# A two-layer graph attention kernel: the loop's order of steps on four engines laid out anew

## Chip, cores and metric

The kernel runs on one NeuronCore of a Trainium2 chip. The metric is the device time of one launch in microseconds (us). Before the change it is 1103.05 us, the median of 3 runs (1102.35 to 1104.42).

## What is computed

Two attention layers over 64 graphs of 128 nodes with 384 features, each followed by a residual sum and a layer norm. The first has 6 heads of 64 and a dot-product softmax; the second has 12 heads of 32 with additive attention, an ELU and a gate.

```python
def _L0_gnn_ref(seq_inputs, Wq, bq, Wk, bk, Wv, bv, Wf, bf, graph_mask):   # 6 heads of 64
    q = _heads(seq_inputs @ Wq + bq)
    k = _heads(seq_inputs @ Wk + bk)
    v = _heads(seq_inputs @ Wv + bv)
    scores = jnp.einsum('bhqd,bhkd->bhqk', q, k) / np.sqrt(HEAD_SIZE)
    bias = jnp.where(graph_mask, 0.0, NEG)[:, None]
    probs = jax.nn.softmax(scores + bias, axis=-1)
    ctx = jnp.einsum('bhqk,bhkd->bhqd', probs, v)
    ...
    return ctx @ Wf + bf

def _L1_gnn_ref(feat_in, adj, W, b, w_src, w_dst, H_w, H_b):               # 12 heads of 32
    h = jnp.einsum('bnd,ade->bane', feat_in, W)
    th = jnp.tanh(h)
    attn_src = jnp.einsum('bane,aeo->bano', th, w_src)
    attn_dst = jnp.einsum('bane,aeo->bano', th, w_dst)
    attn = attn_src + jnp.swapaxes(attn_dst, 2, 3)
    attn = jnp.where(attn >= 0, attn, LEAKY_ALPHA * attn)
    attn = jnp.where(mask, jnp.float32(-999.0), attn)
    attn = jax.nn.softmax(attn, axis=-1)
    feat_out = jnp.einsum('banm,bame->bane', attn, h) + b
    ...
    feat_out = jax.nn.elu(feat_out)
    gate = jax.nn.sigmoid(feat_in @ H_w.T + H_b)
    return gate * feat_out + (1.0 - gate) * feat_in

x = _layernorm(x + _L0_gnn_ref(x, ..., adj), axis=-1)      # x: 64 x 128 x 384, adj: 64 x 128 x 128
x = _layernorm(x + _L1_gnn_ref(x, adj, ...), axis=-1)
```

## The kernel before

The 64 graphs go through in 16 groups of 4. Weights and inputs are split into a high and a low part (the `hi` and `lo` steps), and each projection is 9 matmuls: 3 slices of the features by 3 products of parts (`project`, L577). The work of a group is cut into some 70 named steps on each engine, and every step carries the number of a graph in the group or of a part of one: `("qk", 3)` is the fourth of the six query and key projections, `("wb", 7)` the eighth of twelve blocks of second-layer logits.

The program has three phases: a beginning, a loop of 13 turns (`Fori(1, NG - 2)` with `NG` = 16) and an end. The order in which an engine does its steps is written out by hand in tables: `PE_LOOP`, `ACT_LOOP`, `DVE_LOOP` and `POOL_LOOP` for a turn of the loop, and others for the beginning and the end. In one turn the second layer works on group u, the first layer on group u + 1, and the transposes of the inputs (`xT`, `xhi`, `xlo`) on group u + 2. No engine reorders anything: a step that waits holds up all that stands behind it in its table.

Steps wait for each other by semaphores, one to a kind of step. Besides the data, TensorE (PE) waits for banks. All transposes and the `wb` blocks go to two PSUM banks in turn (`t_bank`, the kinds in `T_STAGES`), all projections to two others (`p_bank`, the kinds in `P_STAGES`). A step takes the bank of the step two places ahead of it among its kinds, so it waits until that one's result was read (`bank`, and the tables `t_freed` and `p_freed`). A change of the order thus also changes who waits for whom.

Steps that the prediction speaks of, with their lines:

- PE: `v`, `qk`, `h`, `gate`, `f` (L577), `xT` (L609), `s` (L639), `pT` (L648), `pv0` (L660), `maskT` (L678), `x1T` (L686), `qwT` (L707), `wb` (L716), `pv1` (L730 and L736), `sumsT` (L750).
- ScalarE (ACT): `qkout` (L801, reads `qk`), `pTo` (L827), `chi` (L833), `hout` (L846, L848), `sumsTo` (L853), `gatet` (L858), `pqw` (L864 to L867), `qwhi` (L876), `qwTo` (L883), `elu` (L890, L894), `exp` (L818), `xhi` (L787).
- VectorE (DVE): `sda` (L1018), `wlog` (L1022), `mixa`, `mixb`, `sum1` (L1064, L1069, L1075), `e` (L1042), `f_raw` (L1057, frees the bank of `sumsT`), and `xlo`, `x1lo`, `clo`, `qwlo`, all by the helper `low` (L920).
- GpSimd (POOL): `prod` (L1142), `rows` (L1149, makes `w_rows` for three `wb`), `norm` (L1130), `fb` (L1154), `ex` (L1160), `rstd` (L1111, L1113).

The second layer's chain for a graph: `h`, `hout`, `prod`, `sd`, `sda`, `wlog`, `pqw`, `qwhi`, `qwlo`, `qwT`, `qwTo`, `rows`, `wb`, `e`, `pv1`, `sumsTo`, `sumsT`, `f_raw`, `fb`, `elu`, `ex`, `mixa`, `mixb`, `sum1`.

Of the kernel before, what the change touches and what calls it, by code (L numbers as in the profile page):

```python
# [25 lines left out]

PE_LOOP = [
# [8 lines left out]
]  # L36

PE_BEGIN = [
# [37 lines left out]
]  # L76

ACT_LOOP = [
    ("vout", 0), ("masks", 0), ("x1hi", 0), ("qkout", 0), ("qkout", 1), ("qkout", 2), ("hout", 0), ("x1hi", 1),
    ("pqw", 0), ("qwhi", 0), ("qkout", 3), ("hout", 1), ("qwTo", 0), ("qkout", 4), ("gatet", 0), ("qkout", 5),  # L80
    ("pqw", 1), ("qwhi", 1), ("x1hi", 2), ("qwTo", 1), ("gatet", 1), ("exp", 0), ("vout", 1), ("hout", 2),
    ("sumsTo", 0), ("x1hi", 3), ("exp", 1), ("elu", 0), ("hout", 3), ("pTo", 0), ("pTo", 1), ("pqw", 2), ("pTo", 2),
    ("qwhi", 2), ("sumsTo", 1), ("pTo", 3), ("pqw", 3), ("chi", 0), ("qwhi", 3), ("qwTo", 2), ("exp", 2), ("vout", 2),
    ("qwTo", 3), ("exp", 3), ("chi", 1), ("pTo", 4), ("pTo", 5), ("vout", 3), ("elu", 1), ("sumsTo", 2), ("gatet", 2),
    ("chi", 2), ("pTo", 6), ("elu", 2), ("sumsTo", 3), ("pTo", 7), ("chi", 3), ("xhi", 0), ("xhi", 1), ("elu", 3),
    ("xhi", 2), ("xhi", 3), ("gatet", 3),
]

# [33 lines left out]
]  # L122

DVE_LOOP = [
    ("x1lo", 0), ("gsum", 0), ("x1lo", 1), ("sd", 0), ("sda", 0), ("wlog", 0), ("qwlo", 0), ("sd", 1), ("sda", 1),
    ("wlog", 1), ("qwlo", 1), ("gsum", 1), ("x1lo", 2), ("mask", 0), ("e", 0), ("max", 0), ("e", 1), ("e", 2),
    ("mask", 1), ("e", 3), ("e", 4), ("e", 5), ("rden0", 0), ("max", 1), ("rden1", 0), ("x1lo", 3), ("f_raw", 0),
    ("sd", 2), ("sda", 2), ("rden0", 1), ("wlog", 2), ("gsum", 2), ("mask", 2), ("max", 2), ("sd", 3), ("sda", 3),
    ("qwlo", 2), ("wlog", 3), ("mixa", 0), ("mixb", 0), ("qwlo", 3), ("sum1", 0), ("rden1", 1), ("clo", 0),
    ("stats1", 0), ("mask", 3), ("mv1", 0), ("rden0", 2), ("f_raw", 1), ("max", 3), ("e", 6), ("e", 7), ("e", 8),  # L130
    ("sum0", 0), ("stats0", 0), ("clo", 1), ("rden0", 3), ("mv0", 0), ("e", 9), ("e", 10), ("e", 11), ("mixa", 1),
    ("rden1", 2), ("f_raw", 2), ("mixb", 1), ("sum0", 1), ("clip", 0), ("clo", 2), ("stats0", 1), ("out", 0),
    ("x1", 0), ("sum1", 1), ("clip", 1), ("mv0", 1), ("stats1", 1), ("sum0", 2), ("mixa", 2), ("rden1", 3),
    ("mv1", 1), ("f_raw", 3), ("mixb", 2), ("clo", 3), ("stats0", 2), ("xlo", 0), ("sum1", 2), ("mv0", 2),
    ("gsum", 3), ("xlo", 1), ("x1", 1), ("stats1", 2), ("sum0", 3), ("xlo", 2), ("mv1", 2), ("xlo", 3), ("mixa", 3),
    ("stats0", 3), ("mixb", 3), ("out", 1), ("mv0", 3), ("sum1", 3), ("stats1", 3), ("mv1", 3), ("out", 2), ("x1", 2),
    ("x1", 3), ("out", 3),
]

# [55 lines left out]
POOL_LOOP = [  # L195
    ("prod", 0), ("prod", 1), ("rows", 0), ("rows", 1), ("x_res", 0), ("prod", 2), ("norm", 0), ("fb", 0),
    ("norm", 1), ("prod", 3), ("ex", 0), ("rows", 2), ("norm", 2), ("rows", 3), ("fb", 1), ("norm", 3), ("ex", 1),
    ("rstd1", 0), ("rstd0", 0), ("fb", 2), ("ex", 2), ("rstd0", 1), ("fb", 3), ("rstd1", 1), ("rstd0", 2), ("ex", 3),
    ("rstd1", 2), ("rstd0", 3), ("rstd1", 3),
]  # L200

# [1009 lines left out]
```

## Time and profile before

| what | us |
|---|---|
| median of 3 runs | 1103.05 |
| the profiled execution, whole | 1102.98 |
| its span, first to last instruction | 1101.1 |
| PE busy | 1057.9 (96%) |
| VectorE busy | 872.4 (79%) |
| GpSimd busy | 704.2 (64%) |
| ScalarE busy | 651.4 (59%) |
| chain that ended last | PE 79%, VectorE 12%, issue 6% |

The span is time from the first to the last instruction; what lies around it is 1.9 us. Busy time of PE is modelled: the records of neighbouring matmuls overlap, and a short wait for a bank does not show as idle time. The distance from the start of one step to the start of the next does show it. The granted clock of TensorE is 1.00 in every turn of the loop. DMA moves 28 GB/s over the span.

### The profile page before, as it was taken

The numbers are of one execution on the slowest core, as the hardware profiler recorded it, in microseconds if no ns is written. First come the engines' busy times: TensorE is split into PE (matmuls) and PEld (weight loads), VectorE is DVE, ScalarE is ACT, GpSimd is POOL, SyncE is SP. The second block draws the span as 40 slices with busy tenths as digits, with TensorE's granted clock in tenths as the row PEclk, the third lists the DMA queues.
The fourth block names the chain that finished last, engine by engine and source line by source line (L and its number), as shares of the span: only waits on it lengthen the run. The fifth ranks groups of instructions, "written<-read, shape, count | busy, mean of one in ns | idle before, by whom it ended". The sixth has DMA issues, their size and how long they took to land.

```text
span 1101.1 us, 28478 instructions
## 1 busy us (share of the span) xinstructions
PE 1057.9 (96%) x9226; PEld 894.6 (81%) x9226; DVE 872.4 (79%) x2289; ACT 651.4 (59%) x2060; POOL 704.2 (64%) x605
## 2 busy tenths in 40 slices
PE   6999999999999999999999999999999999999974
PEld 4888888888888888888888888888888888888853
DVE  3659779696887969789696987969789696977977
ACT  4747466474755647566475755647565575746532
POOL 0347577575766758477575757758577574866765
PEclk9999999999999999999999999999999999999988
DMA  6101010000101001010000101001010100100000
GB/s 189 32 1 33 30 33 9 22 30 29 31 29 31 7 21 31 29 31 14 22 30 21 31 29 31 7 21 31 29 31 19 38 9 21 31 29 2 9 16 37
DMA packets 34722, 31.00 MB, mean 28 GB/s; under 512 B 15872, under 2 KB 34688, under 8 KB 34688
## 3 DMA queue, kind: packets, MB, share of 16 engines
q1 hardware_dynamic: 34688, 30.57, 9.0%
q8 instruction: 19, 0.31, 0.1%
q14 instruction: 15, 0.12, 0.0%
HBM read 17.98 MB, written 12.58 MB: 28 GB/s over the span
## 4 chain that ended last, share of the span: by engine, by line
PE 79%; DVE 12%; issue 6%; ACT 1%; POOL 1%; DMA 0%; DVEq 0%; POOLq 0%; ACTq 0%
PE p_bank L577 50%; PE t_bank L716 4%; PE context L730 4%; DVE weights L1042 4%; PE scores L639 4%; PE context L736 4%; PE t_bank L648 3%; PE context L660 3%; PE t_bank L609 2%; PE t_bank L750 2%; PE t_bank L686 2%; DVE sd L1011 1%; DVE masked L950 1%; DVE neg_max L958 1%; PE t_bank L707 1%
## 5 line engine op out<-in xcount | busy, mean ns | idle before, releaser
L1149 POOL TENSOR_TENSOR w_rows<-qwT,own_head 96x1536 fp32r<-96x1536 f32 x64 | 179.8, 2809 | 87.8 <-ACT qwT L883 87.8
L1042 DVE SCALAR_TENSOR_TENSOR weights<-t_bank,pqw,clip 128x128 f32<-128x128 f32 x768 | 206.5, 343 | 7.4 <-PE t_bank L716 6.7
L1142 POOL TENSOR_TENSOR prod<-th,w_sd 128x768 f32<-128x768 f32 x64 | 118.3, 1848 | 124.9 <-ACT th L846 124.8
L818 ACT ACTIVATE probs<-masked,neg_max 128x128 f32<-128x128 f32 x384 | 148.8, 391 | 46.4 <-DVE neg_max L958 46.4
L577 PE MATMUL p_bank<-xT,w_q 128*128 128x512 f32 x432 | 113.7, 408 | 4.3 <-DVE w_k L927 4.3
L577 PE MATMUL p_bank<-w_v,xT 128*128 128x384 f32 x576 | 115.1, 344 | 1.2 <-DVE clip L995 1.2
L577 PE MATMUL p_bank<-w_f,cT 128*128 128x384 f32 x576 | 115.4, 344 | 0.4 <-DVE cT L920 0.4
L577 PE MATMUL p_bank<-w_h,x1T 128*128 128x384 f32 x576 | 113.8, 342 | 0.2 <-DVE x1T L920 0.2
L577 PE MATMUL p_bank<-w_g,x1T 128*128 128x384 f32 x576 | 113.1, 340 | 0.0
L577 PE MATMUL p_bank<-xT,w_k 128*128 128x512 f32 x432 | 111.4, 402 | 0.0
L1130 POOL TENSOR_TENSOR probs<-probs,rden 128x768 f32<-128x768 f32 x64 | 94.4, 1475 | 25.0 <-DVE rden L963 25.0
L577 PEld LDWEIGHTS p_bank<-w_h,x1T 128*128 128x128 f32 x576 | 101.2, 189 | 6.2 <-issue 2.6
L577 PEld LDWEIGHTS p_bank<-w_v,xT 128*128 128x128 f32 x576 | 99.7, 188 | 5.3 <-issue 3.4
L577 PEld LDWEIGHTS p_bank<-w_g,x1T 128*128 128x128 f32 x576 | 100.9, 188 | 2.0
L577 PEld LDWEIGHTS p_bank<-w_f,cT 128*128 128x128 f32 x576 | 99.0, 188 | 1.7 <-DVE cT L920 1.0
L577 PEld LDWEIGHTS p_bank<-xT,w_q 128*128 128x128 f32 x432 | 80.2, 191 | 24.4 <-DVE w_k L927 4.7
L1154 POOL TENSOR_TENSOR f_b<-f_raw,bias 128x384 f32<-128x384 f32 x64 | 71.3, 1114 | 40.2 <-DVE f_raw L1057 40.1
L1160 POOL TENSOR_TENSOR elu_steps<-elu_steps,x 128x384 f32<-128x384 f32 x64 | 74.9, 1170 | 30.0 <-ACT elu_steps L894 27.2
L1011 DVE TENSOR_REDUCE sd<-prod 128x24 f32<-128x768 f32 x64 | 60.4, 944 | 41.7 <-POOL prod L1142 41.7
L577 PEld LDWEIGHTS p_bank<-xT,w_k 128*128 128x128 f32 x432 | 79.5, 189 | 16.2
L716 PE MATMUL t_bank<-w_rows,qwT 96*128 96x512 f32 x192 | 84.6, 468 | 5.8 <-ACT probs0T L827 2.1
L1113 POOL TENSOR_TENSOR rstd<-ve,minus_half 128x1 f32<-128x1 f32 x128 | 79.1, 618 | 10.0
(109 smaller groups left out, 2279.9 us busy)
## 6 DMA issues: line engine op xcount, KB each, us to landing
x_in<-in_x_dram SPq DMA_DIRECT2D x16, 768.0 KB, 4.7
out_dram<-y_out SPq DMA_DIRECT2D x64, 192.0 KB, 1.9
adj_in<-in_adj_dram SPq DMA_DIRECT2D x16, 64.0 KB, 4.3
probs0T<-in_L_gnn_Wq_dram SPq DMA_DIRECT2D x1, 576.0 KB, 6.2
weights<-in_L_gnn_Wk_dram SPq DMA_DIRECT2D x1, 576.0 KB, 7.3
x_res<-in_L_gnn_Wv_dram SPq DMA_DIRECT2D x1, 576.0 KB, 7.4
probs<-in_L_gnn_Wf_dram SPq DMA_DIRECT2D x1, 576.0 KB, 7.4
x<-in_L_gnn_W_dram SPq DMA_DIRECT2D x3, 192.0 KB, 6.1
```

The source lines that it names most:

```text
L577: last = te.matmul(dst, left(a, kt), right(b, kt), start=(n == 0), stop=(n == 3 * KT - 1))
L639: last = te.matmul(scores[:, b, j * P:(j + 1) * P], head(qT, j, b, k), head(kT, j, b, k), start=True, stop=True)
L716: te.matmul(dst[:, :], qwT[:, g % 2, 0, :], w_rows[0:QW_ROWS, g % 2, heads, :].rearrange("p h i -> p (h i)"), start=True, stop=True).then_ ...
L818: last = act.activation(probs0[:, k % 2, b, j * P:(j + 1) * P], masked[:, k % 2, b * PAIRS + j, :], ACT.Exp, bias=neg_max[:, b * PAIRS + j ...
L1011: dve.tensor_reduce(sd[:].rearrange("p a h -> p (a h)"), prod[:].rearrange("p a (h e) -> p (a h) e", h=H1), AX_X, ALU.add).then_inc(s_sd, 1)
L1042: last = dve.scalar_tensor_tensor(out=weights[:, g % 2, n, :], in0=src[:, i * P:(i + 1) * P], scalar=pqw[:, g % 2, 0, n:n + 1], in1=clip[: ...
L1113: pool.tensor_tensor(rstd, ve, minus_half[:], ALU.pow).then_inc(made_rstd, 1)
L1130: pool.tensor_tensor(probs, probs, per_head(rden0[:], P), ALU.mult).then_inc(s_norm, 1)
L1142: pool.tensor_tensor(prod[:], over_heads(th[:], 2), w_sd[:], ALU.mult).then_inc(s_prod, 1)
L1149: pool.tensor_tensor(w_rows[0:QW_ROWS, k % 2], over_heads(qwT[:, k % 2, 1, :].bitcast(F32), H1), per_head(own_head[:], P), ALU.mult).then_ ...
L1154: pool.tensor_tensor(f_b[:, k % 2, :].rearrange("p (h e) -> p h e", h=H1), f_raw[:].rearrange("p (h e) -> p h e", h=H1), over_heads(bias_1 ...
L1160: pool.tensor_tensor(exp_less_x, f_exp, x1[:, k, :], ALU.subtract).then_inc(s_ex, 1)
```

## The change

No instruction is added, removed or altered. The four loop tables are permuted; those of the beginning and the end stay. The new order was laid out for the mean over four randomly shifted sets of durations. In ACT's table, besides what stands below, `gatet` 1 goes behind `sumsTo` 0, `gatet` 2 ahead of `exp` 3, `pTo` 6 ahead of `chi` 2, and `elu` 3 ahead of `xhi` 1. At PE's end `xT` 2 goes ahead of `f` 3, and in DVE's table `stats1` 2 ahead of `xlo` 1. Some lines of the difference:

```diff
 PE_LOOP = [
...
-    ("qwT", 0), ("qk", 4), ("x1T", 2), ("qk", 5), ("gate", 1), ("s", 0), ("qwT", 1), ("wb", 0), ("v", 1), ("wb", 1),
+    ("qk", 4), ("qwT", 0), ("qk", 5), ("x1T", 2), ("gate", 1), ("s", 0), ("wb", 0), ("qwT", 1), ("v", 1), ("wb", 1),
...
-    ("pv1", 1), ("h", 3), ("pT", 0), ("s", 2), ("pT", 1), ("pT", 2), ("pT", 3), ("pv0", 0), ("s", 3), ("qwT", 2),
-    ("sumsT", 1), ("v", 2), ("qwT", 3), ("f", 0), ("wb", 6), ("wb", 7), ("v", 3), ("wb", 8), ("pv0", 1), ("pT", 4),
+    ("pv1", 1), ("pT", 0), ("h", 3), ("s", 2), ("pT", 1), ("pT", 2), ("pT", 3), ("pv0", 0), ("s", 3), ("sumsT", 1),
+    ("qwT", 2), ("v", 2), ("qwT", 3), ("f", 0), ("wb", 6), ("wb", 7), ("v", 3), ("wb", 8), ("pv0", 1), ("pT", 4),
...
 ACT_LOOP = [
...
-    ("pqw", 0), ("qwhi", 0), ("qkout", 3), ("hout", 1), ("qwTo", 0), ("qkout", 4), ("gatet", 0), ("qkout", 5),
+    ("qkout", 3), ("pqw", 0), ("qwhi", 0), ("hout", 1), ("qwTo", 0), ("qkout", 4), ("qkout", 5), ("gatet", 0),
...
 DVE_LOOP = [
...
-    ("rden1", 2), ("f_raw", 2), ("mixb", 1), ("sum0", 1), ("clip", 0), ("clo", 2), ("stats0", 1), ("out", 0),
+    ("sum0", 1), ("clip", 0), ("rden1", 2), ("mixb", 1), ("f_raw", 2), ("stats0", 1), ("mv0", 1), ("clo", 2),
...
 POOL_LOOP = [
...
-    ("rstd1", 0), ("rstd0", 0), ("fb", 2), ("ex", 2), ("rstd0", 1), ("fb", 3), ("rstd1", 1), ("rstd0", 2), ("ex", 3),
+    ("rstd1", 0), ("rstd0", 0), ("fb", 2), ("ex", 2), ("rstd1", 1), ("fb", 3), ("rstd0", 1), ("ex", 3), ("rstd0", 2),
```

PE, the first quarter of a turn, from `("h", 1)` to the step behind `("s", 0)`. Before:

```order
L577 MATMUL p_bank1<-w_h,x1T 128x384 x9
L707 MATMUL t_bank0<-ident,qw_parts 96x128 x2
L467 REGISTER_ALU
L577 MATMUL p_bank0<-xT,w_q 128x512 x9
L683 REGISTER_ALU
L686 MATMUL t_bank1<-ident,x1 128x128 x3
L577 MATMUL p_bank1<-xT,w_k 128x512 x9
L467 REGISTER_ALU
L577 MATMUL p_bank0<-w_g,x1T 128x384 x9
L634 REGISTER_ALU
L639 MATMUL scores<-kT,qT 128x128 x6
L707 MATMUL t_bank0<-ident,qw_parts 96x128 x2
L716 MATMUL t_bank1<-w_rows,qwT 128x512
```

Now:

```order
L577 MATMUL p_bank1<-w_h,x1T 128x384 x9
L467 REGISTER_ALU
L577 MATMUL p_bank0<-xT,w_q 128x512 x9
L707 MATMUL t_bank0<-ident,qw_parts 96x128 x2
L577 MATMUL p_bank1<-xT,w_k 128x512 x9
L683 REGISTER_ALU
L686 MATMUL t_bank1<-ident,x1 128x128 x3
L467 REGISTER_ALU
L577 MATMUL p_bank0<-w_g,x1T 128x384 x9
L634 REGISTER_ALU
L639 MATMUL scores<-kT,qT 128x128 x6
L716 MATMUL t_bank0<-w_rows,qwT 128x512
```

The transposes of `qw_parts` (`qwT` 0 and 1) each go one matmul step later: the first behind a `qk` projection, the second behind the first block of `w_rows` logits (`wb` 0). With it the banks of these two swap.

VectorE, the middle of a turn: `qw_parts` is `qwlo` (2, then 3), `mix` is `mixa` and `mixb`, `sum1` and `stats1` belong to the first graph's second layer norm. Before (`f_raw` 1 stands three rows behind the last):

```order
L920 TENSOR_TENSOR qw_parts<-pqw,qw_parts 128x2x12
L1022 TENSOR_SCALAR wlog<-sda 128x12
L1064 SCALAR_TENSOR_TENSOR mix<-f_b,elu_steps 128x384
L1069 SCALAR_TENSOR_TENSOR mix<-gate_t,mix 128x384
L1024 REGISTER_ALU
L920 TENSOR_TENSOR qw_parts<-pqw,qw_parts 128x2x12
L1075 SCALAR_TENSOR_TENSOR sum1<-mix,x1 128x384
L1050 RECIPROCAL rden1<-t_bank0 128x4x3
L920 TENSOR_TENSOR cT<-context0,cT 128x384
L1079 BN_STATS stats1<-sum1 128x6
L945 REGISTER_ALU
L950 TENSOR_TENSOR masked<-scores,neg 128x768
```

Now:

```order
L1064 SCALAR_TENSOR_TENSOR mix<-f_b,elu_steps 128x384
L1024 REGISTER_ALU
L920 TENSOR_TENSOR qw_parts<-pqw,qw_parts 128x2x12
L1022 TENSOR_SCALAR wlog<-sda 128x12
L1069 SCALAR_TENSOR_TENSOR mix<-gate_t,mix 128x384
L1050 RECIPROCAL rden1<-t_bank1 128x4x3
L1075 SCALAR_TENSOR_TENSOR sum1<-mix,x1 128x384
L1024 REGISTER_ALU
L920 TENSOR_TENSOR qw_parts<-pqw,qw_parts 128x2x12
L920 TENSOR_TENSOR cT<-context0,cT 128x384
L1057 TENSOR_TENSOR f_raw<-t_bank1,rden1 128x384
```

`mixa` goes ahead of `qwlo` 2, `sum1` ahead of `qwlo` 3, and `f_raw` 1 comes ahead of `stats1`.

PE, the last fifth of a turn, from behind `("pv1", 3)` to `("pv0", 3)`. Before:

```order
L678 MATMUL t_bank1<-ident_b,adj_b 128x128 x2
L467 ISA
L648 MATMUL t_bank0<-ident,probs0 128x128 x3
L577 MATMUL p_bank1<-w_f,cT 128x384 x9
L467 REGISTER_ALU
L750 MATMUL t_bank1<-ident,sumsT 128x128 x4
L652 REGISTER_ALU
L660 MATMUL context0<-probs0T,v 64x128 x6
```

Now:

```order
L648 MATMUL t_bank1<-ident,probs0 128x128 x3
L467 REGISTER_ALU
L678 MATMUL t_bank0<-ident_b,adj_b 128x128 x2
L577 MATMUL p_bank1<-w_f,cT 128x384 x9
L467 REGISTER_ALU
L750 MATMUL t_bank1<-ident,sumsT 128x128 x4
L660 MATMUL context0<-probs0T,v 64x128 x6
```

`pT` 7 and `maskT` 1 swap, so `sumsT` 3 now takes the bank of `pT` 7 and no longer that of `maskT` 1.

## Rows read from the trace of the kernel before

**Rows 1.** The page: span, then busy us (share of the span) xinstructions.
```profile
span 1101.1 us, 28478 instructions
...
PE 1057.9 (96%) x9226; PEld 894.6 (81%) x9226; DVE 872.4 (79%) x2289; ACT 651.4 (59%) x2060; POOL 704.2 (64%) x605
```
**Rows 2.** Stretches: us, PE, PEld, DVE, ACT, POOL busy, clock, DMA share, GB/s.
```profile
451.80:517.60 65.80, 65.13 (x576) 55.35 (x575) 53.67 (x143) 40.20 (x129) 44.04 (x38) 1.00 0.08 25
...
978.00:1101.10 123.10, 101.71 (x904) 82.01 (x901) 97.91 (x259) 57.29 (x179) 77.62 (x68) 0.93 0.05 19
```
**Rows 3.** Timeline, PE, first third: start us, us, instruction, count, [idle <-releaser].
```profile
465.66 1.73 PE L577 MATMUL p_bank<-w_h,x1T 128*128 128x384 f32 x9
467.29 0.42 PE L707 MATMUL t_bank<-ident,qw_parts 128*96 128x128 f32 x2
467.64 2.38 PE L577 MATMUL p_bank<-xT,w_q 128*128 128x512 f32 x9
...
474.82 0.42 PE L707 MATMUL t_bank<-ident,qw_parts 128*96 128x128 f32 x2
475.34 0.47 PE L716 MATMUL t_bank<-w_rows,qwT 96*128 96x512 f32 x1
```
**Rows 4.** Timeline, ACT, the same place.
```profile
466.92 0.67 ACT L801 ACTIVATE kT<-p_bank,bias_q 128x512 f32<-128x512 f32 x1
```
**Rows 5.** Timeline, DVE: the second `sda` of the turn.
```profile
471.02 1.64 DVE L1018 TENSOR_TENSOR sda<-sd,sd_shift 128x24 f32<-128x24 f32 x1
```
**Rows 6.** Timeline, POOL: `rows` 0, 2 and 3, `fb` 1 and 2.
```profile
469.86 2.76 POOL L1149 TENSOR_TENSOR w_rows<-qwT,own_head 96x1536 fp32r<-96x1536 f32 x1
...
494.27 3.00 POOL L1149 TENSOR_TENSOR w_rows<-qwT,own_head 96x1536 fp32r<-96x1536 f32 x1 [2.14 <-ACT qwT L883]
...
498.66 2.75 POOL L1149 TENSOR_TENSOR w_rows<-qwT,own_head 96x1536 fp32r<-96x1536 f32 x1
501.38 1.00 POOL L1154 TENSOR_TENSOR f_b<-f_raw,bias 128x384 f32<-128x384 f32 x1
...
507.73 1.25 POOL L1154 TENSOR_TENSOR f_b<-f_raw,bias 128x384 f32<-128x384 f32 x1 [0.60 <-DVE f_raw L1057]
```
**Rows 7.** Timeline, PE, middle of the turn.
```profile
493.03 0.42 PE L707 MATMUL t_bank<-ident,qw_parts 128*96 128x128 f32 x2
493.29 0.60 PE L750 MATMUL t_bank<-ident,sumsT 128*128 128x128 f32 x4
```
**Rows 8.** Timeline, DVE, the same place.
```profile
492.72 0.18 DVE L920 TENSOR_TENSOR qw_parts<-pqw,qw_parts 128x24 fp32r<-128x24 f32 x1
...
492.91 0.56 DVE L1064 SCALAR_TENSOR_TENSOR mix<-f_b,elu_steps 128x384 f32<-128x384 f32 x1
...
493.98 0.18 DVE L920 TENSOR_TENSOR qw_parts<-pqw,qw_parts 128x24 fp32r<-128x24 f32 x1
494.10 0.56 DVE L1075 SCALAR_TENSOR_TENSOR sum<-mix,x 128x384 f32<-128x384 f32 x1
...
496.61 0.52 DVE L1057 TENSOR_TENSOR f_raw<-t_bank,rden 128x384 f32<-128x384 f32 x1
```
**Rows 9.** Timeline, PE, `qwT` 3, `f` 0 and the two `wb` behind it.
```profile
495.31 0.38 PE L707 MATMUL t_bank<-ident,qw_parts 128*96 128x128 f32 x2
495.45 1.83 PE L577 MATMUL p_bank<-w_f,cT 128*128 128x384 f32 x9
497.32 0.74 PE L716 MATMUL t_bank<-w_rows,qwT 96*128 96x512 f32 x2
```
**Rows 10.** Timeline, ACT, last `probs0T` copy of the turn.
```profile
510.63 0.48 ACT L827 ACTIVATE probs0T<-t_bank 128x384 f32<-128x384 f32 x1
```
**Rows 11.** Timeline, PE, end of the turn: `sumsT` 3, then `xT` 2 and 3.
```profile
511.60 0.60 PE L750 MATMUL t_bank<-ident,sumsT 128*128 128x128 f32 x4
...
516.82 0.82 PE L609 MATMUL t_bank<-ident,x_in 128*128 128x128 f32 x6
```
**Rows 12.** Timeline, DVE, `xlo` 1.
```profile
516.38 0.55 DVE L920 TENSOR_TENSOR xT<-t_bank,xT 128x384 fp32r<-128x384 f32 x1
```

More of the change, by code:

```diff
@@ L78 @@
 ACT_LOOP = [
-    ("vout", 0), ("masks", 0), ("x1hi", 0), ("qkout", 0), ("qkout", 1), ("qkout", 2), ("hout", 0), ("x1hi", 1),
-    ("pqw", 0), ("qwhi", 0), ("qkout", 3), ("hout", 1), ("qwTo", 0), ("qkout", 4), ("gatet", 0), ("qkout", 5),
[L81 to L85, printed above, removed]
+    ("x1hi", 0), ("vout", 0), ("qkout", 0), ("masks", 0), ("qkout", 1), ("qkout", 2), ("hout", 0), ("x1hi", 1),
+    ("qkout", 3), ("pqw", 0), ("qwhi", 0), ("hout", 1), ("qwTo", 0), ("qkout", 4), ("qkout", 5), ("gatet", 0),
+    ("pqw", 1), ("x1hi", 2), ("qwhi", 1), ("qwTo", 1), ("exp", 0), ("vout", 1), ("hout", 2), ("sumsTo", 0),
+    ("gatet", 1), ("x1hi", 3), ("exp", 1), ("elu", 0), ("hout", 3), ("pTo", 0), ("pTo", 1), ("sumsTo", 1), ("pqw", 2),
+    ("pTo", 2), ("pTo", 3), ("qwhi", 2), ("chi", 0), ("pqw", 3), ("qwhi", 3), ("qwTo", 2), ("exp", 2), ("qwTo", 3),
+    ("vout", 2), ("gatet", 2), ("exp", 3), ("chi", 1), ("pTo", 4), ("pTo", 5), ("vout", 3), ("elu", 1), ("sumsTo", 2),
+    ("pTo", 6), ("chi", 2), ("elu", 2), ("sumsTo", 3), ("pTo", 7), ("chi", 3), ("xhi", 0), ("elu", 3), ("xhi", 1),
     ("xhi", 2), ("xhi", 3), ("gatet", 3),
@@ L124 @@
 DVE_LOOP = [
-    ("x1lo", 0), ("gsum", 0), ("x1lo", 1), ("sd", 0), ("sda", 0), ("wlog", 0), ("qwlo", 0), ("sd", 1), ("sda", 1),
-    ("wlog", 1), ("qwlo", 1), ("gsum", 1), ("x1lo", 2), ("mask", 0), ("e", 0), ("max", 0), ("e", 1), ("e", 2),
-    ("mask", 1), ("e", 3), ("e", 4), ("e", 5), ("rden0", 0), ("max", 1), ("rden1", 0), ("x1lo", 3), ("f_raw", 0),
+    ("x1lo", 0), ("x1lo", 1), ("gsum", 0), ("sd", 0), ("sda", 0), ("wlog", 0), ("qwlo", 0), ("sd", 1), ("sda", 1),
+    ("wlog", 1), ("gsum", 1), ("x1lo", 2), ("qwlo", 1), ("mask", 0), ("e", 0), ("max", 0), ("e", 1), ("e", 2),
+    ("mask", 1), ("e", 3), ("rden0", 0), ("e", 4), ("e", 5), ("max", 1), ("rden1", 0), ("x1lo", 3), ("f_raw", 0),
     ("sd", 2), ("sda", 2), ("rden0", 1), ("wlog", 2), ("gsum", 2), ("mask", 2), ("max", 2), ("sd", 3), ("sda", 3),
-    ("qwlo", 2), ("wlog", 3), ("mixa", 0), ("mixb", 0), ("qwlo", 3), ("sum1", 0), ("rden1", 1), ("clo", 0),
-    ("stats1", 0), ("mask", 3), ("mv1", 0), ("rden0", 2), ("f_raw", 1), ("max", 3), ("e", 6), ("e", 7), ("e", 8),
-    ("sum0", 0), ("stats0", 0), ("clo", 1), ("rden0", 3), ("mv0", 0), ("e", 9), ("e", 10), ("e", 11), ("mixa", 1),
-    ("rden1", 2), ("f_raw", 2), ("mixb", 1), ("sum0", 1), ("clip", 0), ("clo", 2), ("stats0", 1), ("out", 0),
[L133 to L136, printed above, removed]
+    ("mixa", 0), ("qwlo", 2), ("wlog", 3), ("mixb", 0), ("rden1", 1), ("sum1", 0), ("qwlo", 3), ("clo", 0),
[4 rows of a table added]
+    ("rden1", 3), ("f_raw", 3), ("mixb", 2), ("clo", 3), ("xlo", 0), ("stats0", 2), ("sum1", 2), ("gsum", 3),
+    ("stats1", 2), ("xlo", 1), ("mv0", 2), ("xlo", 2), ("x1", 1), ("mv1", 2), ("sum0", 3), ("xlo", 3), ("mixa", 3),
+    ("stats0", 3), ("mixb", 3), ("out", 1), ("x1", 2), ("sum1", 3), ("mv0", 3), ("out", 2), ("stats1", 3), ("mv1", 3),
     ("x1", 3), ("out", 3),
```

11 rows, old and new, of tables (DVE_LOOP, PE_LOOP) are left out of this document.

## The prediction

> **What bounds it.** I read the page first: the span is 1101.1 us and TensorE (PE) is busy for 1057.9 of it, 96% [rows 1]. Nothing else is near that, and PE does not get less work, so the change can give back only what PE waits. The table of stretches comes next: a turn of the loop takes 65.80 us at a granted clock of 1.00, and the 13 turns are 855 us of the span; the rest, like the 123.1 us behind the loop, keeps its order [rows 2]. Busy time cannot show the short waits, so I went through one turn in the timeline and took the distance from each step's start to the next one's. Where two steps of one kind differ there, the longer one holds a wait. For example `qwT` 3 (at 495.31) lets `f` 0 start 0.14 us later, while `qwT` 0 (467.29) holds the next step back for 0.35 and `qwT` 1 (474.82) for 0.52 [rows 3, 9]. I found about 2.7 us of such waits in a turn. All of them gone would be 13 x 2.7 = 35 us, the ceiling. The question is how many go and how many come back elsewhere.
>
> **The change, place by place.** Each term is us per turn.
>
> First third, `qk` 4. It starts at 467.64, 0.05 behind the end of the `kT` copy that frees its bank (466.92 + 0.67 = 467.59) [rows 3, 4]. ScalarE makes that copy behind `pqw` 0 and `qwhi` 0, though its input was there at about the start of `h` 1, 465.66. Now `qkout` 3 goes ahead of these two, and `qk` 4 goes straight behind `h` 1. `qwT` 0 sits between two projections and should cost 0.14 instead of 0.35, and `h` 1 no longer ends in a wait for `qwlo` 0 (under 0.1). Bounds: -0.21 (the transpose alone) and -0.4 (with the refill behind a wait at `qk` 4). I take -0.3. `qwlo` 0 and `qwTo` 0 come later, and `rows` 0 with them by about 0.4, but `wb` 0 starts at 475.34 and `rows` 0 ended at 472.62 [rows 3, 6], so 2.7 us cover it.
>
> `wb` 0 and `qwT` 1. The 0.38 that `qwT` 1 holds too long is a wait for `x1lo` 2, which frees the bank of `wb` 0. In the new order `wb` 0 fills most of that time, but `qwlo` 1 now comes behind `x1lo` 2 on VectorE, so `qwT` 1 waits for it instead, and `wb` 1 takes the bank of `wb` 0 and so waits for `e` 0. One wait becomes two shorter ones. Between -0.3 (all hidden) and +0.3 (both last as long as the old one); I take 0.
>
> Middle, `qwT` 2 to `wb` 6. `mixa` 0 goes ahead of `qwlo` 2, which moves that 0.5 us back (a `mix` is 0.56 long, with 0.1 overlapped) [rows 8]. Before, `qwT` 2 started at 493.03, 0.13 behind the end of `qwlo` 2 (492.90), and `sumsT` 1 followed at 493.29 [rows 7, 8]; now `sumsT` 1 goes first and fills the time, so `qwT` 2 comes about where it was. Then `qwT` 3 takes the bank of `sumsT` 1, which `f_raw` 1 frees. Before, `f_raw` 1 ended at 497.13, 1.8 behind the start of `qwT` 3 [rows 8, 9]. It is moved ahead of `stats1`, `mask` 3, `mv1` and `rden0`, 1.5 us of work, so it ends at about 495.2 to 495.6, while PE would be ready for `qwT` 3 at 494.9 to 495.0. That is a new wait of 0.2 to 0.6. It costs less than that, because `f` 0 to `wb` 6 is 1.87 where a 384-wide projection needs 1.6 to 1.7: there PE waited for `rows` 2, which ended at 497.27, 0.05 ahead of `wb` 6 at 497.32 [rows 6, 9]. The two waits share one slack. `rows` 2 itself took 3.00 against 2.75 for `rows` 3 [rows 6]; it ran beside `sum1` 0 (494.10 to 494.66) [rows 8], which reads two tiles of SBUF, and now `sum1` 0 starts about 0.5 ahead of it. So `wb` 6 can come 0.3 earlier, or 0.2 later if `f_raw` 1 comes at the late end. I take -0.15.
>
> From `wb` 6 to `f` 1 PE's order is the same. VectorE gets to `max` 3 some 0.1 to 0.2 sooner, as `mv1` 0 goes behind `e` 8, and the `wb` and `pT` blocks here wait for `e` and for `pTo`: 0 to -0.25, I take -0.1.
>
> End, `sumsT` 3. It takes the bank of `pT` 7, so it now waits for the last `probs0T` copy. That ended at 511.11, and `sumsT` 3 started at 511.60 [rows 10, 11]: 0.49 of slack. Two things move it. `f_raw` 2 goes behind `sum0` 1, `clip` 0 and `mixb` 1, about 1.3 us of steps, of which VectorE's idle time ahead of the old place and its head start cover 0.8 to 1.0; and the chain `fb` 2, `elu` 2, `sumsTo` 3, `pTo` 7 hangs on it. Against it, `fb` 2 took 1.25 beside `mixb` 1 where `fb` 1 took 1.00 [rows 6], and it no longer runs beside `mixb`. The copy then ends at 511.1 to 511.6 on the old clock, while PE with its gains would be there at 511.1. Cost 0 to +0.5; I take +0.2.
>
> Seam, `xT` 3. It waits for `xlo` 1, which ended at 516.93, while `xT` 2 and 3 started at 516.82 and some 0.33 later [rows 11, 12]. VectorE now does `stats1` 2 ahead of `xlo` 1, and ScalarE does `elu` 3 ahead of `xhi` 1. Slack of 0.2 against a delay of 0 to 0.5: 0 to +0.3, I take +0.05.
>
> **Sum.** -0.3 + 0 - 0.15 - 0.1 + 0.2 + 0.05 = -0.3 us a turn, times 13 is -3.9. The profiled execution is 1102.98 us, its span and 1.9 around it, and 0.07 under the median of 1103.05. So 1102.98 - 3.9 = 1099.1 us. This forecast holds for -0.1 to -0.45 a turn, 1097.1 to 1101.7. All terms at their best ends are -1.25 (1086.7) and all at their worst +1.1 (1117.3), but a PE that comes late at one place waits less at the next, so neither sum is likely.
>
> **A collision that could turn it.** VectorE's second `sda` of a turn has 24 elements a row and took 1.64 us [rows 5], where a `qw_parts` of the same size takes 0.18 [rows 8]. It ended at 472.66, 0.04 behind the end of `rows` 0 at 472.62 [rows 5, 6]. So a VectorE instruction with two operands in SBUF that comes while a large GpSimd one runs is held until that one's end. `qwlo` reads two tiles in SBUF too. In the new order `qwlo` 3 stands behind `sum1` 0 and comes at almost the same moment as `rows` 2 starts: before, `qwlo` 3 began at 493.98 and `rows` 2 at 494.27, 0.29 later [rows 6, 8]; `sum1` 0 in front moves it back by 0.46, so now they are within 0.1 of each other. If `rows` 2 is first, `qwlo` 3 waits for up to 2.75 us, and `qwT` 3, `f` 0 and all behind it with it.
> The Trainium skill (SBUF — State Buffer, section "SBUF: two separate sides") calls the pair of ports that the two engines share an exclusive lock: whichever starts first has it for its whole instruction and the other fully blocks. The trace agrees for `sda`, 1.64 against 0.18. By that rule a start of `rows` 2 ahead of `qwlo` 3 makes the slow case below, 1132 us.
> What speaks against it: `sum1` 0 starts well before `rows` 2 and the next VectorE instruction follows it with no gap, so VectorE may keep the port through both.
>
> **Rivals.**
> 1. The end gives it back. `sumsT` 3 waits for `pTo` 7 and `xT` 3 for `xlo` 1, both in full: +0.5 and +0.3 in place of +0.2 and +0.05 makes -0.3 + 0.55 = +0.25; with the shared slack between the two taken off, about +0.1 a turn, 1104.3, and 1101.7 to 1106 as its range. For it: ScalarE's order at that place is `elu`, `sumsTo`, `pTo` with nothing to overtake. Against: the shorter `fb` 2.
> 2. The waits in the middle go further than I take: `wb` 1, `qwT` 3 and `wb` 6 all at their better ends, -0.6 a turn, 1095.2. For it: the ceiling is 2.7. Against: each has a new releaser only a little ahead.
> 3. The collision at `qwlo` 3, the slower side. `rows` 2 ends 2.75 after its start, `qwT` 3 comes at about 497.1 instead of 495.3, and `clo` 0, `f_raw` 1 and the whole of VectorE's work behind it are late by 2.5. PE loses 2.0 to 2.6 a turn: 13 x 2.3 = 30, less the 1 us or so of gain ahead of it, 1132. It decides on whether `rows` 2 starts before `qwlo` 3.
>
> That the tables would not do what they say is excluded: each engine's order is the table's.
>
> **Chances.** Forecast 0.40, rival 1 0.33, rival 2 0.17, rival 3 0.10. About 0.2%, 2.2 us, is what a measurement of this kernel can tell from no change, so faster means below 1100.8 and slower above 1105.3. Faster: 0.34 of the forecast's 0.40 and all of rival 2, 0.51. Same: 0.06 and 0.20 of rival 1, 0.26. Slower: 0.13 of rival 1 and rival 3, 0.23. The range 1094.5 to 1108 takes in the forecast, rival 1 and the nearer part of rival 2; it leaves out rival 3.
>
> **What would show it.** The stretch of one turn should be 65.5 instead of 65.80, with a clock of 1.00 as before. `h` 1 to `qk` 4 should be 1.6 with no wait, and `qwT` 0 0.14 long. `qwT` 3 should start within 0.1 of the end of `f_raw` 1, and `rows` 2 take 2.75 to 2.85. `sumsT` 3 should start either right behind the last `probs0T` copy (rival 1) or clear of it. A `qwlo` of over 1 us anywhere is rival 3. I am wrong if the turn is above 65.7 with `sumsT` 3 clear of its copy, or if the difference lies outside the 13 turns.

## The result, and the profile after

The changed kernel takes 1106.43 us (median of 20 runs, 1105.07 to 1108.19), the kernel before 1102.94 on the same chip (20 runs). The ratio is 1.0031 with a 95% interval of 1.0024 to 1.0038: slower by 0.31%, where 0.35% faster was forecast (1102.98 to 1099.1). The profiled execution has a span of 1104.5 us.

The page after, span and busy times, against [rows 1]:
```profile
span 1104.5 us, 28473 instructions
...
PE 1061.7 (96%) x9221; PEld 890.1 (81%) x9226; DVE 875.1 (79%) x2289; ACT 656.7 (59%) x2060; POOL 682.5 (62%) x605
```
The table of stretches after (columns as in [rows 2]), the same turn and the part behind the loop:
```profile
452.90:518.96 66.06, 65.45 (x574) 54.99 (x574) 53.85 (x143) 40.56 (x128) 42.32 (x38) 1.00 0.08 25
981.30:1104.50 123.20, 101.11 (x898) 81.94 (x901) 97.51 (x259) 57.01 (x178) 76.59 (x68) 0.94 0.05 19
```
A turn is 66.06 us instead of 65.80, and the part behind the loop 123.2 instead of 123.1. The loss is in the 13 turns: 13 x 0.28 = 3.6 us. Below, "turn" is the mean of the last ten: 65.78 before, 66.06 after. The last of them leads into the end phase and is some 0.2 shorter (65.61 and 65.84), so the turns in the middle of the loop are 65.80 and 66.08. POOL is busy for 22 us less and the time is not shorter for it.

To see where in the turn, I took the start of each TensorE step behind the start of its turn's `v` 0 (median over the last ten turns) and cut the turn at steps that stand in the same place in both orders:

| stretch | predicted | before | after | difference |
|---|---|---|---|---|
| turn start to `h` 1 | 0 | 13.90 | 13.90 | 0.00 |
| `h` 1 to `s` 0 | -0.3 | 8.29 | 8.01 | -0.28 |
| `s` 0 to `wb` 3 | 0 | 6.38 | 6.51 | +0.13 |
| `wb` 3 to `s` 3 | 0 | 11.63 | 11.55 | -0.08 |
| `s` 3 to `wb` 6 | -0.15 | 5.35 | 5.51 | +0.16 |
| `wb` 6 to `f` 1 | -0.1 | 7.30 | 7.20 | -0.10 |
| `f` 1 to `sumsT` 3 | +0.2 | 6.98 | 7.09 | +0.11 |
| `sumsT` 3 to the next turn | +0.05 | 5.95 | 6.29 | +0.34 |

The eight differences sum to +0.28, where -0.3 was forecast.

The first third did what was forecast. The timeline of TensorE after, against [rows 3]: `qk` 4 straight behind `h` 1, `qwT` 0 only 0.13 ahead of `qk` 5; then `wb` 0 and `qwT` 1.
```profile
468.36 2.26 PE L577 MATMUL p_bank<-xT,w_q 128*128 128x512 f32 x9
470.46 0.38 PE L707 MATMUL t_bank<-ident,qw_parts 128*96 128x128 f32 x2
470.59 2.35 PE L577 MATMUL p_bank<-xT,w_k 128*128 128x512 f32 x9
...
475.65 0.50 PE L716 MATMUL t_bank<-w_rows,qwT 96*128 96x512 f32 x1
476.18 0.42 PE L707 MATMUL t_bank<-ident,qw_parts 128*96 128x128 f32 x2
```
`qwT` 1 starts at 476.18, 0.06 behind the end of `qwlo` 1 in VectorE's timeline after (475.95 + 0.17 = 476.12), and `sda` 1, held by `rows` 0 before for 1.64 [rows 5], is now held for 2.13, again until the end of `rows` 0 (471.42 + 2.75 = 474.17):
```profile
472.09 2.13 DVE L1018 TENSOR_TENSOR sda<-sd,sd_shift 128x24 f32<-128x24 f32 x1
...
475.95 0.17 DVE L920 TENSOR_TENSOR qw_parts<-pqw,qw_parts 128x24 fp32r<-128x24 f32 x1
```
Middle of the turn after, against [rows 7 to 9]. TensorE (`v` 2, `qwT` 3, `f` 0):
```profile
494.56 1.83 PE L577 MATMUL p_bank<-w_v,xT 128*128 128x384 f32 x9
496.57 0.39 PE L707 MATMUL t_bank<-ident,qw_parts 128*96 128x128 f32 x2 [0.17 <-DVE f_raw L1057]
496.72 1.81 PE L577 MATMUL p_bank<-w_f,cT 128*128 128x384 f32 x9
```
VectorE, the same place (`sum1` 0, `qwlo` 3, and behind `clo` 0 `f_raw` 1), and POOL's `rows` 2:
```profile
494.86 0.53 DVE L1075 SCALAR_TENSOR_TENSOR sum<-mix,x 128x384 f32<-128x384 f32 x1
495.31 0.18 DVE L920 TENSOR_TENSOR qw_parts<-pqw,qw_parts 128x24 fp32r<-128x24 f32 x1
...
495.87 0.55 DVE L1057 TENSOR_TENSOR f_raw<-t_bank,rden 128x384 f32<-128x384 f32 x1
```
```profile
495.38 2.75 POOL L1149 TENSOR_TENSOR w_rows<-qwT,own_head 96x1536 fp32r<-96x1536 f32 x1 [2.32 <-ACT qwT L883]
```
`qwT` 3 waits for `f_raw` 1, as the brackets say. `qwlo` 3 began 0.07 ahead of `rows` 2 and took 0.18: the collision did not happen, by 0.07 us. The margin is 0.07 in all 13 turns. Both steps hang on the same one, `wlog` 3 (494.18): `qwlo` 3 follows it on VectorE after 1.13, `rows` 2 by way of ScalarE (`pqw` 3, `qwhi` 3, `qwTo` 2) after 1.20. `rows` 2 took 2.75 as forecast.

The end, ScalarE's last `probs0T` copy (`pTo` 7) and TensorE's `sumsT` 3, which starts 0.18 behind the end of that copy (511.99 + 0.48 = 512.47):
```profile
511.99 0.48 ACT L827 ACTIVATE probs0T<-t_bank 128x384 f32<-128x384 f32 x1
```
```profile
512.65 0.60 PE L750 MATMUL t_bank<-ident,sumsT 128*128 128x128 f32 x4
```

The seam after, against [rows 11, 12]. TensorE (`xT` 2, `f` 3, `xT` 3, next turn's `v` 0), VectorE (`gsum` 3, `stats1` 2, `xlo` 1) and ScalarE (`elu` 3 in two rows, then `xhi` 1 and 2 in one):
```profile
516.53 1.81 PE L577 MATMUL p_bank<-w_f,cT 128*128 128x384 f32 x9
518.38 0.55 PE L609 MATMUL t_bank<-ident,x_in 128*128 128x128 f32 x3
518.97 1.85 PE L577 MATMUL p_bank<-w_v,xT 128*128 128x384 f32 x9
```
```profile
516.85 0.55 DVE L1005 TENSOR_TENSOR gate_sum<-p_bank,gate_bias 128x384 f32<-128x384 f32 x1
517.31 0.55 DVE L1079 BATCH_NORM_STATS2 stats<-sum 128x6 f32<-128x384 f32 x1
517.78 0.54 DVE L920 TENSOR_TENSOR xT<-t_bank,xT 128x384 fp32r<-128x384 f32 x1
```
```profile
516.04 0.62 ACT L890 ACTIVATE elu_steps<-f_b,minus_one 128x384 f32<-128x384 f32 x1 [0.90 <-POOL f_b L1154]
516.69 0.53 ACT L894 ACTIVATE elu_steps<-elu_steps 128x384 f32<-128x384 f32 x1
517.12 0.86 ACT L787 ACTIVATE xT<-t_bank 128x384 fp32r<-128x384 f32 x2
```
`xT` 3 starts at 518.38, 0.06 behind the end of `xlo` 1 (518.32). From `f` 3 to `xT` 3 it is 1.85 and from `xT` 3 to `v` 0 0.59. VectorE has no idle bracket here (one is printed from 0.15 us on): it is one unbroken run.

### The profile page after: what moved, and what is told of

Read it like the earlier page. It is cut to its first block, busy times and chain, and to the rows that moved or that the text cites. A ratio compares the mean times of both kernels' runs of the same rounds, so it can differ in the third digit from the quotient of the medians.

```text
span 1104.5 us, 28473 instructions
## 1 busy us (share of the span) xinstructions
PE 1061.7 (96%) x9221; PEld 890.1 (81%) x9226; DVE 875.1 (79%) x2289; ACT 656.7 (59%) x2060; POOL 682.5 (62%) x605
## 4 chain that ended last, share of the span: by engine, by line
PE 82%; DVE 10%; issue 5%; ACT 1%; POOL 1%; DMA 0%; DVEq 0%; POOLq 0%; ACTq 0%
PE p_bank L577 51%; PE t_bank L716 5%; PE context L730 4%; DVE weights L1042 4%; PE scores L639 4%; PE context L736 4%; PE t_bank L648 3%; PE context L660 2%; PE t_bank L609 2%; PE t_bank L750 2%; PE t_bank L686 2%; PE t_bank L707 1%; DVE sd L1011 1%; DVE masked L950 1%; DVE f_raw L1057 1%
## 5 line engine op out<-in xcount | busy, mean ns | idle before, releaser
L1149 POOL TENSOR_TENSOR w_rows<-qwT,own_head 96x1536 fp32r<-96x1536 f32 x64 | 176.6, 2759 | 93.1 <-ACT qwT L883 93.1
L1154 POOL TENSOR_TENSOR f_b<-f_raw,bias 128x384 f32<-128x384 f32 x64 | 68.2, 1066 | 53.9 <-DVE f_raw L1057 53.7
L827 ACT ACTIVATE probs0T<-t_bank 128x384 f32<-128x384 f32 x128 | 61.0, 491 | 55.0 <-PE t_bank L648 53.8
L920 DVE TENSOR_TENSOR x1T<-t_bank,x1T 128x384 fp32r<-128x384 f32 x64 | 34.9, 545 | 74.0 <-ACT x1T L839 73.1
L1160 POOL TENSOR_TENSOR elu_steps<-elu_steps,x 128x384 f32<-128x384 f32 x64 | 66.5, 1040 | 35.7 <-ACT elu_steps L894 33.4
```

What stands on the lines that cost most here:

```text
L827: act.activation(probs0T[:, g % 2, b, :], t_bank[t_at("pT", k, turn)][:, 0:PAIRS * P], ACT.Copy).then_inc(s_pT, 1)
L1149: pool.tensor_tensor(w_rows[0:QW_ROWS, k % 2], over_heads(qwT[:, k % 2, 1, :].bitcast(F32), H1), per_head(own_head[:], P), ALU.mult).then_ ...
L1154: pool.tensor_tensor(f_b[:, k % 2, :].rearrange("p (h e) -> p h e", h=H1), f_raw[:].rearrange("p (h e) -> p h e", h=H1), over_heads(bias_1 ...
L1160: pool.tensor_tensor(exp_less_x, f_exp, x1[:, k, :], ALU.subtract).then_inc(s_ex, 1)
```

## The experiments

All were timed beside the kernel before, in four groups (its medians there: 1102.41, 1102.27, 1102.84 and 1102.87). Ratios are to it, with 95% intervals; a ratio is not the quotient of the two medians printed and differs from it by up to 0.0014. The intervals are about 0.2% wide, so small effects are read from the turn in the profile. An edit is given as the piece of the table that it changes.

**The seam, one half at a time.**
```diff
 DVE_LOOP (on the kernel after)
-("gsum", 3), ("stats1", 2), ("xlo", 1), ("mv0", 2),
+("gsum", 3), ("xlo", 1), ("stats1", 2), ("mv0", 2),
```


> The changed kernel with one step moved: stats1 2 goes behind xlo 1 again on VectorE. The turn of the changed kernel is 66.08 us, of the kernel before 65.80. Theory A (each new releaser costs its own wait): xT 3 no longer waits for xlo 1; f 3 to xT 3 falls from 1.85 to 1.68 and xT 3 to the next turn's v 0 from 0.59 to 0.42, so the turn is 65.75 and the time 4 us under the changed kernel, 1102. Theory B (VectorE's whole chain of steps sets the turn, and a wait taken away at one place comes back at the next): the turn stays within 0.05 of 66.08.

Measured: 1105.86, ratio 1.0032 [1.0021, 1.0042], turn 66.01. `xlo` 1 now waited for ScalarE instead. `f` 3 to `xT` 3 fell from 1.85 to 1.72, but `xT` 3 to `v` 0 kept its 0.59, and `qk` 0 started 0.09 later behind `v` 0 (2.02), as `xlo` 3 ended at 1.89. VectorE after this edit:
```profile
517.86 0.56 DVE L920 TENSOR_TENSOR xT<-t_bank,xT 128x384 fp32r<-128x384 f32 x1 [0.24 <-ACT xT L787]
```
`xhi` 1 is held by `elu` 3, which waited for `fb` 3. Taking this one of the two blockers away is worth 0.05. The other half alone was not run; the unbroken run of VectorE shown above, with `stats1` 2 right ahead of `xlo` 1, is what speaks for it gaining no more.

```diff
 PE_LOOP (on the kernel after)
-("xT", 1), ("xT", 2), ("f", 3), ("xT", 3),
+("xT", 1), ("f", 3), ("xT", 2), ("xT", 3),
```


> The changed kernel with PE's f 3 ahead of xT 2 again; VectorE's and ScalarE's orders as changed. Theory A: xT 3 comes 0.33 behind xT 2 instead of behind f 3, at about 65.35 + 0.1, and still waits for xlo 1 (65.45), but the way from xT 3 to the next turn is 0.42 to 0.59: turn 65.9 to 66.1, time 0 to 2 us under the changed kernel. If the long way to v 0 (0.59) comes of xT 3 standing alone behind a projection and not of its wait, the turn is 65.9; if it comes of the wait, 66.05. Theory B: 66.08.

Measured: 1110.2, ratio 1.0072 [1.0058, 1.0085], turn 66.30. That is above both theories. With the old order of TensorE over the new ones of VectorE and ScalarE, `xT` 3 waits right behind `xT` 2, and `qk` 0 starts 2.16 behind `v` 0 instead of 1.93, behind `xlo` 3 (2.03). `xT` 3 to `v` 0 is 0.59 here too, with `xT` 2 in front of it again, where it was 0.42 before: the long way comes with the wait, not with the place in the order. TensorE's part of the change suits the other two, and undoing it alone costs 0.24 more.

```diff
 DVE_LOOP and ACT_LOOP (on the kernel after)
-("gsum", 3), ("stats1", 2), ("xlo", 1), ("mv0", 2),
+("gsum", 3), ("xlo", 1), ("stats1", 2), ("mv0", 2),
-("xhi", 0), ("elu", 3), ("xhi", 1),
+("xhi", 0), ("xhi", 1), ("elu", 3),
```


> The changed kernel with both steps that hold xlo 1 moved back: stats1 2 behind xlo 1 on VectorE and elu 3 behind xhi 1 on ScalarE (with the first move alone xlo 1 began right behind xhi 1). xlo 1 should end at about 64.95 in the turn, 0.3 ahead of xT 3. Theory A (waits cost what they last, place by place): f 3 to xT 3 is 1.67 and xT 3 to v 0 falls from 0.59 to 0.42; turn 65.75, 1102. Theory B (VectorE runs without a gap from mixa 2 to xlo 3, and that run sets when qk 0 of the next turn may start): xT 3 is free, but qk 0 waits 0.2 to 0.3 for xlo 3 and the turn is 65.95 to 66.0.

Measured: 1103.42, ratio 1.0008 [0.9999, 1.0017], turn 65.89, between the two theories. `xT` 3 no longer waits: `f` 3 to `xT` 3 is 1.66, `xT` 3 to `v` 0 0.33, together 0.45 less. But `qk` 0 now waits for `xlo` 3, which ends 2.03 behind `v` 0, and starts at 2.16: 0.23 goes back.

**The middle.**
```diff
 DVE_LOOP (on the kernel after)
-("qwlo", 3), ("clo", 0), ("f_raw", 1),
+("qwlo", 3), ("f_raw", 1), ("clo", 0),
```


> The changed kernel with f_raw 1 one step further ahead on VectorE, in front of clo 0. Theory A: qwT 3, which waits for f_raw 1, starts 0.35 us earlier in the turn (43.35 instead of 43.70), wb 6 is then held by rows 2 at 45.32 instead of 45.49: turn 65.9, 2 us under the changed kernel. Theory B: wb 6 comes earlier but the gain is gone by the end of the turn: 66.05 to 66.08.

Measured: 1105.31, ratio 1.0030 [1.0018, 1.0042], turn 66.00. `v` 2 to `qwT` 3 fell from 2.00 to 1.67 and `wb` 6 came 0.19 earlier, but the turn fell by 0.06. Half of the 0.19 was gone at once: `wb` 6 now waits for `rows` 2 (494.09 + 2.75 = 496.84), and behind that wait `wb` 7 follows after 0.33 instead of 0.24 (a refill), so `wb` 7 and `f` 1 came only 0.10 earlier. Another 0.04 went at the seam, where `xT` 3 waits for VectorE. POOL (`rows` 2) and TensorE (`wb` 6 and 7) after this edit:
```profile
494.09 2.75 POOL L1149 TENSOR_TENSOR w_rows<-qwT,own_head 96x1536 fp32r<-96x1536 f32 x1 [2.33 <-ACT qwT L883]
```
```profile
496.90 0.73 PE L716 MATMUL t_bank<-w_rows,qwT 96*128 96x512 f32 x2
```

**The first third alone.**
```diff
 PE_LOOP and ACT_LOOP (on the kernel before)
-("h", 1), ("qwT", 0), ("qk", 4), ("x1T", 2), ("qk", 5),
+("h", 1), ("qk", 4), ("qwT", 0), ("qk", 5), ("x1T", 2),
-("pqw", 0), ("qwhi", 0), ("qkout", 3),
+("qkout", 3), ("pqw", 0), ("qwhi", 0),
```


> The kernel before with the first third of the change alone: on PE qwT 0 behind qk 4, on ScalarE qkout 3 ahead of pqw 0. Theory A: h 1 to s 0 is 8.0 us instead of 8.29, and the turn 65.5 instead of 65.80 if nothing later takes it back: 3.7 us under the kernel before, 1099.3. Theory B: s 0 comes 0.28 earlier but the turn stays 65.75 to 65.80, as the waits for rows 2, pTo 4 and pTo 5 grow by the same amount: 0 to 0.6 us.

Measured: 1101.84, ratio 0.9989 [0.9980, 0.9998], turn 65.675, between the two theories. `s` 0 comes 0.30 earlier, but `qwT` 1 to `wb` 0 is 0.70 instead of 0.52 and only 0.11 is left of it. Here `sda` 1 was held for 2.13, until `rows` 0 ended:
```profile
470.53 2.13 DVE L1018 TENSOR_TENSOR sda<-sd,sd_shift 128x24 f32<-128x24 f32 x1
```
```profile
469.86 2.75 POOL L1149 TENSOR_TENSOR w_rows<-qwT,own_head 96x1536 fp32r<-96x1536 f32 x1 [0.45 <-ACT qwT L883]
```

**Is the hold of `sda` 1 what costs it?** To the last kernel one wait was added, so that `rows` 0 starts behind `sda` 1.
```diff
                 elif name == "rows":
                     pool.wait_ge(s_qwT, upto(g1, GROUP, k + 1))
+                    if turn[0] == "loop" and k == 0: pool.wait_ge(s_sda, upto(g1, GROUP, 2))
```


> The kernel before with the first third of the change (turn 65.68) and one more wait, in the loop only: rows 0 on GpSimd waits for sda 1 on VectorE, so that sda 1 runs before rows 0 and is not held by it. rows 0 then ends at about 22.2 instead of 21.3, ahead of wb 0 (23.5). Theory C (what took back 0.2 of the 0.29 us gained by qk 4 is the hold of sda 1: rows 0 now starts 0.45 later and holds sda 1 until 21.3): sda 1 takes 0.2 instead of 2.13, qwlo 1 ends before 21, x1lo 2 at 23.1, wb 0 starts at 23.15 instead of 23.47, and the turn is 65.4 to 65.5. Theory B (VectorE's and ScalarE's later chains set the turn): turn 65.6 to 65.68.

Measured: 1101.34, ratio 0.9987 [0.9978, 0.9995], turn 65.69: nothing gained on the kernel without the wait, and the theory that the hold of `sda` 1 takes the gain back fell. `sda` 1 took 0.18, and `qwlo` 1 was held in its place, until `rows` 0 ended (471.00 + 2.75 = 473.75; 472.89 + 0.91 = 473.80). It ended 22.41 behind the turn's start, against 22.37 without the wait, so what a free `qwlo` 1 would be worth is not shown by this run:
```profile
470.58 0.18 DVE L1018 TENSOR_TENSOR sda<-sd,sd_shift 128x24 f32<-128x24 f32 x1
...
472.89 0.91 DVE L920 TENSOR_TENSOR qw_parts<-pqw,qw_parts 128x24 fp32r<-128x24 f32 x1 [1.91 <-ACT qw_parts L876]
```
```profile
471.00 2.75 POOL L1149 TENSOR_TENSOR w_rows<-qwT,own_head 96x1536 fp32r<-96x1536 f32 x1 [1.53 <-DVE sda L1018]
```

**The collision, made to happen.**
```diff
 DVE_LOOP (on the kernel after)
-("sum1", 0), ("qwlo", 3), ("clo", 0), ("f_raw", 1), ("stats1", 0),
+("sum1", 0), ("clo", 0), ("f_raw", 1), ("qwlo", 3), ("stats1", 0),
```


> The changed kernel with qwlo 3 two steps later on VectorE, behind clo 0 and f_raw 1, so that rows 2 starts on GpSimd (42.5) before qwlo 3 (43.5). If a VectorE instruction with two operands in SBUF is held until a running GpSimd one ends: qwlo 3 takes until the end of rows 2, some 1.8 us instead of 0.18, qwT 3 comes at about 45.4 instead of 43.7, and the turn is 67.3 to 68.3, 1122 to 1135. If it is not held: qwlo 3 ends at 43.6, ahead of qwT 3, and the turn stays at 66.08.

Measured: 1135.02, ratio 1.0289 [1.0276, 1.0302], turn 68.33. `qwlo` 3, 0.18 long otherwise, took 1.93 and ended 0.04 behind `rows` 2 (506.23 + 2.75 = 508.98), and TensorE stood for 1.83. Not all of the 2.27 a turn is this wait: a turn in which the granted clock stays at 1.00 takes 67.78, which is 1.70 more, and the rest is a fall of the clock in 5 of the 13 turns (last section). VectorE (`f_raw` 1, `qwlo` 3), POOL (`rows` 2) and TensorE (`qwT` 3, `f` 0):
```profile
506.62 0.55 DVE L1057 TENSOR_TENSOR f_raw<-t_bank,rden 128x384 f32<-128x384 f32 x1
507.09 1.93 DVE L920 TENSOR_TENSOR qw_parts<-pqw,qw_parts 128x24 fp32r<-128x24 f32 x1
```
```profile
506.23 2.75 POOL L1149 TENSOR_TENSOR w_rows<-qwT,own_head 96x1536 fp32r<-96x1536 f32 x1 [2.32 <-ACT qwT L883]
```
```profile
509.07 0.63 PE L707 MATMUL t_bank<-ident,qw_parts 128*96 128x128 f32 x2 [1.83 <-DVE qw_parts L920]
509.36 3.23 PE L577 MATMUL p_bank<-w_f,cT 128*128 128x384 f32 x9
```
`f_raw` 1, with its large operand in PSUM, ran beside `rows` 2 in its usual 0.55.

**Both repairs.** The kernel after with `f_raw` 1 ahead of `clo` 0 and both halves of the seam undone (the edits of the fourth and third experiment above).

> The changed kernel with f_raw 1 ahead of clo 0, stats1 2 behind xlo 1 and elu 3 behind xhi 1. Theory A: 0.35 at qwT 3 and 0.35 at the seam come off in full or nearly: turn 65.5 to 65.6. Theory B: the two moves together bring no more than 0.1 to 0.15: turn 65.9 to 66.0.

Measured: 1103.47, ratio 1.0003 [0.9994, 1.0012], turn 65.79, 0.27 less than the kernel after: all of its loss, and level with the kernel before. That lies between the two theories. The middle alone gave 0.06 and the seam alone 0.17, so the two repairs nearly add up. `qk` 0 still waits for `xlo` 3.

**VectorE's run at the seam.** On that kernel:
```diff
 DVE_LOOP
-("xlo", 1), ("stats1", 2), ("mv0", 2), ("xlo", 2), ("x1", 1), ("mv1", 2), ("sum0", 3), ("xlo", 3), ("mixa", 3),
+("xlo", 1), ("x1", 1), ("mv0", 2), ("xlo", 2), ("sum0", 3), ("xlo", 3), ("stats1", 2), ("mv1", 2), ("mixa", 3),
```


> e8 with VectorE's order behind `xlo` 1 changed: `x1` 1, `mv0` 2, `xlo` 2, `sum0` 3, `xlo` 3, and `stats1` 2 and `mv1` 2 only then. In e8 `xlo` 3 ended 2.04 us behind the next turn's `v` 0 and `qk` 0 waited for it (2.16 behind `v` 0 instead of 1.93); e8's turn was 65.79. Theory (VectorE's run of steps behind `xlo` 1 now sets the seam): `xlo` 3 ends some 0.6 earlier, `qk` 0 starts 1.93 behind `v` 0, and the turn is 65.79 - 0.23 = 65.56, 13 x 0.22 = 2.9 us under the kernel before, 1099.5, ratio 0.997. Rival (VectorE has no idle time left in the last third, so a step put off there comes back at the next wait): `stats1` 2, `mv1` 2 and what follows them are late instead, a later step of PE in the next turn waits for it, and the turn stays within 0.05 of 65.79, ratio 1.000.

Measured: 1100.78, ratio 0.9972 [0.9958, 0.9985], turn 65.545 (65.56 expected). VectorE, without the edit and with it. The last row of each is `xlo` 3: 2.02 and 1.43 behind the start of `v` 0 (517.38 and 516.09):
```profile
517.30 0.56 DVE L920 TENSOR_TENSOR xT<-t_bank,xT 128x384 fp32r<-128x384 f32 x1
517.77 0.47 DVE L988 TENSOR_SCALAR x<-sum,mv,rstd 128x384 f32<-128x384 f32 x1
518.16 0.17 DVE L1083 BATCH_NORM_AGGREGATE mv<-stats 128x2 f32<-128x6 f32 x1
518.38 0.56 DVE L973 TENSOR_TENSOR sum<-p_bank,x_res 128x384 f32<-128x384 f32 x1
518.85 0.55 DVE L920 TENSOR_TENSOR xT<-t_bank,xT 128x384 fp32r<-128x384 f32 x1
```
```profile
516.03 0.56 DVE L920 TENSOR_TENSOR xT<-t_bank,xT 128x384 fp32r<-128x384 f32 x1
516.51 0.55 DVE L973 TENSOR_TENSOR sum<-p_bank,x_res 128x384 f32<-128x384 f32 x1
516.97 0.55 DVE L920 TENSOR_TENSOR xT<-t_bank,xT 128x384 fp32r<-128x384 f32 x1
```
TensorE's `qk` 0, without the edit and with it: 519.53 - 517.38 = 2.15 behind `v` 0, and 518.03 - 516.09 = 1.94.
```profile
519.53 0.73 PE L577 MATMUL p_bank<-xT,w_q 128*128 128x512 f32 x2
```
```profile
518.03 1.18 PE L577 MATMUL p_bank<-xT,w_q 128*128 128x512 f32 x4
```
The rival (the put-off steps cost as much later) fell: `stats1` 2 and `mv1` 2 had slack.

**Behind `s` 0.** The first third alone, with:
```diff
 DVE_LOOP
-("qwlo", 1), ("gsum", 1), ("x1lo", 2), ("mask", 0),
+("qwlo", 1), ("x1lo", 2), ("gsum", 1), ("mask", 0),
```


> e4 (the kernel before with the first third of the change alone) with VectorE's `x1lo` 2 ahead of `gsum` 1. In e4 `x1lo` 2 was ready to start at 22.55 (its input ended at 22.54) and started at 22.77 behind `gsum` 1, ended at 23.32, and `wb` 0 started at 23.46 behind it; the turn was 65.675. Theory: `wb` 0 starts 0.2 earlier, `mask` 0 and `e` 0 stay where they are, so `wb` 1 (which waits for PE, not for `e` 0, here) moves up too: turn 65.48, 1099.1 us, ratio 0.9965. Rival: `e` 0 is what the next steps wait for, since it stands behind `mask` 0 whatever comes ahead of it, and PE gives 0.1 to 0.2 back at `wb` 1 to `wb` 3: turn 65.6 to 65.68, ratio 0.998 to 0.999.

Measured: 1101.21, ratio 0.9971 [0.9959, 0.9983], turn 65.555: 0.12 gained where 0.2 was there to be had. `wb` 0, `wb` 3 and `wb` 4 came 0.18 earlier, but `pv1` 0 only 0.11: `wb` 4 and `pv1` 0 both want `e` 2, which comes behind `gsum` 1 now and ends 0.08 ahead of `wb` 4, and `wb` 4 to `pv1` 0 is 0.41 instead of 0.33.

**Both together.** The kernel of "VectorE's run at the seam" with the old order behind `s` 0 and `x1lo` 2 ahead of `gsum` 1; in the second form with `wb` 2 behind `s` 1 as well.
```diff
 PE_LOOP, ACT_LOOP and DVE_LOOP
-("s", 0), ("wb", 0), ("qwT", 1),
+("s", 0), ("qwT", 1), ("wb", 0),
-("pqw", 1), ("x1hi", 2), ("qwhi", 1),
+("pqw", 1), ("qwhi", 1), ("x1hi", 2),
-("wlog", 1), ("gsum", 1), ("x1lo", 2), ("qwlo", 1),
+("wlog", 1), ("qwlo", 1), ("x1lo", 2), ("gsum", 1),
 PE_LOOP, second form only
-("wb", 2), ("s", 1),
+("s", 1), ("wb", 2),
```


> e9 and in the first third `qwT` 1 again ahead of `wb` 0, `qwlo` 1 again right behind `wlog` 1 and `qwhi` 1 behind `pqw` 1, with `x1lo` 2 ahead of `gsum` 1 as in e10. From `s` 0 to `wb` 3 it was 6.38 before and 6.50 in e8. Theory: this stretch is 6.35 and the seam as in e9: turn 65.56 - 0.15 = 65.41, 13 x 0.37 = 4.8 us under the kernel before, 1097.6, ratio 0.9956. Rival (both moves are given back, as in the rivals of e9 and e10): turn 65.7, ratio 0.999.

> e11 with PE's `wb` 2 behind `s` 1 again, as in the kernel before. In e11 `wb` 2 waited for `e` 0 (which ended at 25.51, `wb` 2 at 25.58) with `s` 1 queued behind it, so `s` 0 to `wb` 3 was 6.63; in e10, where `s` 1 goes first, it was 6.38. Theory: the stretch is 6.38 here too and the seam stays as in e9 (`qk` 0 at 1.93): turn 65.70 - 0.25 = 65.45, 13 x 0.33 = 4.3 us under the kernel before, 1098.5, ratio 0.996. Rival (a step of PE later in the turn, `pT` 1 or `qwT` 2, stands waiting for VectorE, whose run starts from `mask` 0 at 23.53 whatever PE does here): it stays at 65.55 to 65.60, ratio 0.9975.

Measured: first form 1101.30, ratio 0.9977 [0.9968, 0.9987], turn 65.70 (`wb` 2 waits for `e` 0, and `s` 1 behind it). Second form 1099.12, ratio 0.9968 [0.9957, 0.9980], turn 65.53: the lowest median here, but by the turn only 0.01 under the kernel of "VectorE's run at the seam", and its interval overlaps with that one's and with that of "Behind `s` 0", so no order among the three is shown. `s` 0 to `wb` 3 was 6.39 as expected, and `s` 3 stood at 39.94 in both. VectorE's `gsum` 1, `mask` 0 and the `e` behind them, first in the kernel of "VectorE's run at the seam", then in the second form:
```profile
472.56 0.56 DVE L1005 TENSOR_TENSOR gate_sum<-p_bank,gate_bias 128x384 f32<-128x384 f32 x1 [0.45 <-PE p_bank L577]
473.14 0.56 DVE L920 TENSOR_TENSOR x1T<-t_bank,x1T 128x384 fp32r<-128x384 f32 x1
...
473.70 0.95 DVE L950 TENSOR_TENSOR masked<-scores,neg 128x768 f32<-128x768 f32 x1
```
```profile
472.06 0.56 DVE L920 TENSOR_TENSOR x1T<-t_bank,x1T 128x384 fp32r<-128x384 f32 x1 [0.21 <-ACT x1T L839]
472.54 0.55 DVE L1005 TENSOR_TENSOR gate_sum<-p_bank,gate_bias 128x384 f32<-128x384 f32 x1
473.00 0.95 DVE L950 TENSOR_TENSOR masked<-scores,neg 128x768 f32<-128x768 f32 x1
```
In the first, `gsum` 1 fills time in which VectorE would wait for `x1hi` 2. In the second that time stays idle and `mask` 0 starts 23.56 behind the turn's start instead of 23.17; the run behind it, up to `max` 1, is late by as much, and `wb` 4 and `wb` 5 wait for `e` 2 and `e` 3 (0.08 and 0.06 behind their ends). So the rival held there. The two medians are 1.7 us apart, taken on different chips, and the turns explain 0.2 of it. In the profiles the loop begins anywhere from 121.5 to 122.9 us, over kernels with the same tables ahead of it, so the rest can be such scatter; it is not settled.

## Why the prediction was wrong

**Right.** The first third (-0.28 against -0.3), and that the page's shares say nothing here. The waits that were forecast came where they were forecast: `qwT` 1 behind `qwlo` 1, `wb` 1 behind `e` 0, `qwT` 3 behind `f_raw` 1, `rows` 2 down to 2.75.

**Right by luck.** `wb` 6 to `f` 1 came out at -0.10 as taken, but not by an earlier `max` 3. From `wb` 7 to `f` 1 it is 6.96 before, after, and with the middle repaired. The 0.10 is all at `wb` 6 to `wb` 7, which is 0.34 where `wb` 6 has waited for `rows` 2 (before) and 0.24 where it comes too late to wait (after); with the middle repaired `wb` 6 waits again and the 0.10 is gone. `sumsT` 3 started 0.18 clear of the `probs0T` copy; +0.2 was taken and +0.11 came, not as a wait but in the transposes, whose order changed ahead of it.

Two steps failed, by about 0.3 us a turn each.

**The step that failed: "Seam, `xT` 3"**, taken as +0.05, measured +0.34. It named the right releaser, `xlo` 1, and had slack against delay. Two things were missing. First, two causes pushed it, `stats1` 2 on VectorE and `elu` 3 on ScalarE: undoing the first alone gave 0.05 a turn, undoing both freed `xT` 3 and gave 0.17. Second, a wait at the turn's last transposes costs twice. The next step starts late behind them as well: `xT` 3 to `v` 0 is 0.59 when `xT` 3 has waited, even if it waited for only 0.06, and 0.33 when not (0.42 before, with `xT` 2 in front). I had priced such a refill at `qk` 4 and forgot it here. So the term was 0.18 at `f` 3 and 0.17 at `v` 0.

**The other step that failed: "Middle"**, taken as -0.15, measured +0.16. The new wait at `qwT` 3 was 0.33, inside the 0.2 to 0.6 forecast, and `qwT` 2's side came out at +0.03. Against it stands the old wait at `wb` 6, 0.22 (`f` 0 to `wb` 6, 1.87 down to 1.65), and no more than that could be paid back there. The prediction had this slack too, 1.87 less 1.6 to 1.7, so by its own figures the best end was 0.2 - 0.27 = -0.07, and neither -0.3 nor -0.15 was in reach: an earlier and shorter `rows` 2 was counted as a gain of its own beside the one slack. `clo` 0 ahead of `f_raw` 1 is what made the wait; without it `wb` 6 was 0.19 earlier.

**The step "`wb` 0 and `qwT` 1"**, taken as 0, measured +0.13, inside its bounds; the stretch behind it, which had no term, gave 0.08 back. `x1lo` 2 can't end earlier than `x1hi` 2 lets it: with `gsum` 1 out of its way it waited 0.21 for ScalarE.

**What was under all three.** I treated each wait of TensorE as its own account. They are tied in two ways. One is the refill, the late start of the step behind one that has waited, as at `xT` 3 and `wb` 6. The other is VectorE. It is busy for 82% of a turn (53.85 of 66.06), and from `mask` 3 to `xlo` 3, some 23.6 us, it is idle for only 0.5 in the turn read (0.4 before), so a step that is late there leaves `xlo` 3 late, and `qk` 0 waits for it. That is shown at the seam: with `xT` 3 free `qk` 0 began to wait, and with two steps taken out from ahead of `xlo` 3 that wait went and the turn fell by another 0.25. That the middle's loss travels by this road is not shown; its repair gave 0.06 alone and 0.10 with the seam repaired. The 0.58 between the forecast and the measured turn is the middle (0.31), the seam (0.29) and `wb` 0 (0.13), less what came out better elsewhere. The forecast said that it would be wrong if the turn was above 65.7 with `sumsT` 3 clear of its copy, and that is what came. Rival 1 had the right sign and half of the mechanism (`xT` 3, not `pTo` 7), and the measured time lies just above its range of 1101.7 to 1106.

**The collision (rival 3)** did not strike, by 0.07 us, but it is real. Made to happen, it put `qwT` 3 at 45.33 behind the turn's start, where the prediction has it too (497.1 less 451.8). It cost 2.27 a turn, where 2.3 was taken, but that agreement is luck: the wait itself costs 1.70, below the 2.0 to 2.6 forecast, and a fall of TensorE's clock, which the prediction did not have, makes up the rest. By the Trainium skill (SBUF — State Buffer, section "SBUF: two separate sides") one engine holds the shared pair of ports for its whole instruction; the traces agree in four places (1.93, 2.13, 1.64 and 0.91, each until the end of a `rows`, against 0.18).

## What to carry to other kernels

Where one engine is the bound and another is nearly full, look at the second one's unbroken runs: find the last step of each run for which the first one waits, and keep out of its way everything that has slack (here `stats1` 2 and `mv1` 2, worth 0.25 us a turn). Put a movable step where that engine would be idle anyway, and not where it only makes the next wait of the bound look better. When several steps share a wait, check that each of its causes goes; half a repair of the seam gave 0.05 of 0.17. Price a wait of the bound engine with the late start of the step behind it (here 0.1 to 0.26 us), and pay no more back from a slack than it holds.

## What had not been expected of the hardware

**A wait of 1.83 us can cost more than itself.** In the kernel with the forced collision TensorE's granted clock fell behind the wait, though TensorE was busy for 43.44 of the 45.33 us up to its end. The table of stretches for TensorE (length, busy, granted clock, DMA share, GB/s), up to the end of the wait and, 0.9 later, behind it:
```profile
463.74:509.07 45.33, 43.44 (x344) 1.00 0.10 32
...
509.97:512.40 2.43, 2.43 (x10) 0.50 0.00 0
```
At 0.50 (1.2 GHz) it was 3.0 from `f` 0 to `wb` 6 instead of 1.66, and this turn was 69.38 long; the next one, with the same wait of 1.83 and no fall, 67.78. That stretch was long (2.7 to 3.0) in 5 of the 13 turns, and the wait was 1.83 or 1.84 in all 13. What decides in which is open.

**A hold moves on.** With `rows` 0 put off by 1.1 us, `sda` 1 was free and `qwlo` 1, 2.3 us later, was caught by the same instruction. A small delay of the GpSimd instruction only chose another VectorE instruction to be held; both orders have to be looked at over the whole 2.75 us.
